# All loops of a five-engine kernel (GRU and selective scan over images) written out as straight code

## What is computed

```python
x = x + _L0_conv_ref(_gn(x), Wx, bx, Wh, bh, Wp)          # a GRU over the 196 positions
x = x + _L1_conv_ref(_gn(x), in_proj_w, conv_w, ...)      # a selective scan in 4 directions
# L0, at each of 196 positions, for all 32 images at once:
h_zrn = h @ Wh.T + bh
z = sigmoid(x_z + h_z); r = sigmoid(x_r + h_r)
ncand = tanh(x_n + r * h_n)
h = (1.0 - z) * ncand + z * h
# L1, in each of 4 directions, 192 channels, 16 states:
h = h * exp(d_t * A) + (d_t * u_t) * B_t ;  y = sum over states of h * C_t
```

## Time and profile before

| | us |
|---|---|
| median of three runs | 3238.71 (3237.17 to 3238.81) |
| the profiled execution's own time | 3240.27 |
| its span, first to last instruction | 3238.3 |
| TensorE busy in matmuls / weight loads | 2779.2 (86%) / 2070.2 (64%) |
| VectorE busy | 2672.7 (83%) |
| GpSimd busy | 2243.0 (69%) |
| ScalarE busy | 1824.2 (56%) |

### The profile page before, as it was taken

The page is one execution under the profiler, slowest core; times in us unless marked ns, Lnnn a source line. Parts: engine busy times, 40 slices in busy tenths (PEclk is TensorE's granted clock), DMA queues, the critical chain, the costliest instruction groups (busy, mean ns, idle before and its releaser), DMA issues.

```text
span 3238.3 us, 101526 instructions
## 1 busy us (share of the span) xinstructions
PE 2779.2 (86%) x39496; PEld 2070.2 (64%) x39496; DVE 2672.7 (83%) x4226; ACT 1824.2 (56%) x3872; POOL 2243.0 (69%) x1878
## 2 busy tenths in 40 slices
PE   4999999999996788888888888888888888888886
PEld 4999999986664555555555555565555655656554
DVE  6444444445776999999999999999999999999995
ACT  1111111112224677777777777777777777777773
POOL 5333333320005989989899898888989898898983
PEclk9999999999997999999999999999999999999999
DMA  5000000002334555545545555455454554555541
GB/s 199 0 0 0 0 0 0 0 5 97 112 112 140 156 156 153 153 156 149 177 140 163 159 144 169 141 160 174 134 170 149 157 163 140 162 161 155 162 146 46
DMA packets 57085, 385.29 MB, mean 119 GB/s; under 512 B 10100, under 2 KB 15060, under 8 KB 31700
## 3 DMA queue, kind: packets, MB, share of 16 engines
q1 hardware_dynamic: 57044, 384.79, 38.8%
HBM read 352.64 MB, written 32.11 MB: 119 GB/s over the span
## 4 chain that ended last, share of the span: by engine, by line
DVE 30%; PE 25%; issue 23%; POOL 16%; ACT 3%; DMA 1%; DVEq 1%; POOLq 0%; SPq 0%; ACTq 0%
DVE arena L776 15%; PE ps L1112 10%; PE ps L1121 9%; POOL arena L495 9%; DVE arena L779 9%; PE ps L1108 2%; DVE arena L793 1%; DVE conv_out L203 1%; POOL arena L471 1%; POOL arena L464 1%; POOL arena L468 1%; DVEq L773 1%; DMA x_in<-x_pair 1%; POOL arena L477 1%; POOL arena L482 1%
## 5 line engine op out<-in xcount | busy, mean ns | idle before, releaser
L1244 PE MATMUL ps<-arena,ident 128*128 128x392 f32 (+1 forms) x4096 | 1163.0, 417 | 0.9 <-DVE arena L788 0.9
L963 ACT ACTIVATE ps<-arena,abias,a 128x390 f32<-128x390 f32 x1024 | 690.0, 677 | 317.4 <-DVE arena L779 179.8
L788 DVE TENSOR_TENSOR arena<-arena,ps 128x784 f32<-128x784 f32 x768 | 745.7, 971 | 38.2 <-PE ps L1234 12.8
L1244 PEld LDWEIGHTS ps<-arena,ident 128*128 128x128 f32 x4096 | 682.8, 191 | 143.9 <-DVE arena L788 1.2
L776 DVE TENSOR_TENSOR_SCAN arena<-ps,arena 128x392 f32<-128x392 f32 x768 | 702.6, 956 | 7.4 <-POOL arena L495 6.3
L779 DVE TENSOR_TENSOR_SCAN arena<-ps,arena 128x392 f32<-128x392 f32 x768 | 702.6, 956 | 0.0
L1234 PE MATMUL ps<-arena,sel 96*128 96x196 bf16 x3072 | 391.6, 250 | 355.7 <-DVE arena L788 355.7
L1234 PEld LDWEIGHTS ps<-arena,sel 96*128 96x128 bf16 x3072 | 227.5, 97 | 665.0 <-DVE arena L788 630.7
L967 ACT ACTIVATE ps<-arena,abias,a 128x195 f32<-128x195 f32 x1024 | 477.7, 505 | 254.2 <-DVE arena L776 139.8
L495 POOL TENSOR_TENSOR arena<-arena 128x784 f32<-128x784 f32 x256 | 472.7, 1851 | 102.6 <-PE ps L1244 97.3
L495 POOL TENSOR_TENSOR arena<-arena,wx_sb 128x784 f32<-128x784 f32 x256 | 465.4, 1850 | 14.4 <-POOL arena L482 13.7
(11 more groups left out here) (175 smaller groups left out, 3295.4 us busy)
## 6 DMA issues: line engine op xcount, KB each, us to landing
wx_sb<-b_by_state SPq DMA_DIRECT2D x64, 1568.0 KB, 6.3
wh_sb<-b_by_state SPq DMA_DIRECT2D x64, 1568.0 KB, 6.3
arena<-b_by_image SPq DMA_DIRECT2D x128, 784.0 KB, 9.1
arena<-x_seq SPq DMA_DIRECT2D x4, 2352.0 KB, 15.9
x_in<-x_pair SPq DMA_DIRECT2D x16, 588.0 KB, 4.2
x_dram<-x SPq DMA_DIRECT2D x16, 588.0 KB, 2.8
x<-x_dram SPq DMA_DIRECT2D x16, 588.0 KB, 10.0
out<-xhat SPq DMA_DIRECT2D x16, 588.0 KB, 2.8
```

Of the source, the lines that this page charges most:

```text
L788: dve.tensor_tensor(h, h, bank(3), ALU.mult).then_inc(s["readout_ready"], 1)
L963: ins = act.activation(r, src, ACT.Exp, scale=a01[:, c:c + 1], bias=abias01[:, c:c + 1])
L1244: mm = pe.matmul(ps[:, 5 if g < 8 else 6, 0:cols], ident[:, :], h[:, m * cols:(m + 1) * cols], start=(opens and m == 0), stop=(closes and ...
```

## The change

In all fourteen places a loop on the engine becomes a loop of Python, so each round is put into the program as its own instructions: four loops of the recurrence (97 or 98 rounds, two steps each), a loop on each of the five engines in the middle stage (13 to 15 rounds) and one on each in the scan (14 rounds). `i` is then a number, the waits compare with constants, the addresses are constants, and branches and register instructions are gone. The operations, their order on each engine, the buffers and the waits are the same. With numbers alone, three helpers lose their second form.

```diff
@@ sync
-            with sp.Fori(2, PAIRS) as i:
+            for i in range(2, PAIRS):
...
-            with nc.Fori(1, PAIRS - 1, engines=[sp.engine], hint_back_edge=True) as i:
+            for i in range(1, PAIRS - 1):
                 pair(i, False, False)
@@ gpsimd
             def tok(t):
-                return seq[:, :, bass.ds(t, 1)].rearrange("p c o -> p (c o)") if not isinstance(t, int) else seq[:, :, t]
+                return seq[:, :, t]
...
-            with pool.Fori(0, T // 2 - 1) as i:
+            for i in range(0, T // 2 - 1):
                 for p in range(2):
                     norm(i * 2 + (p + 2), p)
                     keep(i * 2 + p, p)
...
-            with pool.Fori(1, PAIRS) as i:
+            for i in range(1, PAIRS):
                 rstd_c(i)
@@ vector
-            with dve.Fori(1, T // 2) as i:
+            for i in range(1, T // 2):
                 for p in range(2):
                     step(i * 2 + p, p)
...
-            with dve.Fori(2, PAIRS) as i:
+            for i in range(2, PAIRS):
                 norm_and_convolve(i)
@@ scalar
-            with act.Fori(0, T // 2) as i:
+            for i in range(0, T // 2):
                 for p in range(2):
                     step(i * 2 + p, p)
...
-            with act.Fori(3, PAIRS) as i:
+            for i in range(3, PAIRS):
                 conv_silu(i - 2)
                 xh_and_z(i - 1)
                 normalise(i)
@@ tensor
-            with pe.Fori(0, T // 2 - 1) as i:
+            for i in range(0, T // 2 - 1):
                 for p in range(2):
                     step(i * 2 + p, p)
...
-                        rhs = seq[:, col:col + 2, :] if isinstance(i, int) else seq[:, bass.ds(col, 2), :]
+                        rhs = seq[:, col:col + 2, :]
...
-            with pe.Fori(2, PAIRS) as i:
+            for i in range(2, PAIRS):
                 project(i)
@@ helper
 def dram(t, i):
-    return t[i] if isinstance(i, int) else t[bass.ds(i, 1), :, :].rearrange("o p c -> (o p) c")
+    return t[i]
```

More of the change, by code:

```diff
@@ L535, in _ @@
             pair(0, True, False)
-            with nc.Fori(1, PAIRS - 1, engines=[pool.engine], hint_back_edge=True) as i:
+            for i in range(1, PAIRS - 1):
                 pair(i, False, False)
@@ L807, in _ @@
             pair(0, True, False)
-            with nc.Fori(1, PAIRS - 1, engines=[dve.engine], hint_back_edge=True) as i:
+            for i in range(1, PAIRS - 1):
                 pair(i, False, False)
@@ L1071, in _ @@
             pair(0, True, False)
-            with nc.Fori(1, PAIRS - 1, engines=[act.engine], hint_back_edge=True) as i:
+            for i in range(1, PAIRS - 1):
                 pair(i, False, False)
@@ L1373, in _ @@
             pair(0, True, False)
-            with nc.Fori(1, PAIRS - 1, engines=[pe.engine], hint_back_edge=True) as i:
+            for i in range(1, PAIRS - 1):
                 pair(i, False, False)
```

## The result

The straight kernel takes 3391.91 us (median of four runs, 3390.32 to 3393.77) against 3238.19 (3237.17 to 3238.81, four runs of before on the same chip): ratio 1.0475, 95% interval 1.0457 to 1.0493. That is +153.7 us, where +138 was forecast. The profiled execution took 3392.38 us, +152.1 on that of before.

| stretch | before | after | change | forecast |
|---|---|---|---|---|
| start to the end of the recurrence | 719.3 | 882.0 | +162.6 | +145 |
| middle stage, to the first scan | 303.5 | 301.4 | -2.1 | -5 |
| the 16 pairs of the scan | 2180.1 | 2173.9 | -6.2 | -2 |
| tail after the last scan | 35.4 | 33.2 | -2.2 | none |

A forecast was written before the change was run, and what follows sets the result against it. The prediction took TensorE to bound the recurrence, with VectorE busy 1874.9 of the scan's 1909.7 us. Terms 145 - 5 - 2 = +138 us on 3238.7 gave 3377 us; range 3300 to 3430, held at 0.80.

The forecast's parts named there:

- Recurrence, fetch: Recurrence on TensorE: 225 instruction blocks fetched one after another, 3.63 us each, 817 us in place of 671.7: +145 us.
- The upper end (3.88): Recurrence: slowest block spacing allowed for, 3.88 us, giving 873 us for 225 blocks, +201.
- Recurrence, branches: Recurrence: 97 branches of 0.05 us saved would be 5 us, but counted as 0 where fetches set the pace.
- Middle stage: 14 looped rounds: the load of x issues sooner without branch and registers, 14 x 0.35 = -5 us.
- Scan: 14 looped pairs and the last pair: shorter VectorE idle spots, together -2 us; ends -13 and +25.
- The 0.08 of L788: Scan: VectorE's first wait for TensorE in a looped pair falls from 0.29 to 0.21 us, 14 x 0.08 = -1 us.
- VectorE's spot of 0.88 us: Scan, last pair: idle time after "issue", read as a late VectorE block after the loop; should go, -1 us.
- rival 3: Recurrence fetch-bound and VectorE's block boundaries in the scan cost +25 in place of -2: 3404 us; within fetch-bound's 0.84.
- Rivals 1: Recurrence: fetches keep up with TensorE, so only savings of 12 us stay: 3227 us, faster; chance 0.09.
- 2 (3241): Recurrence: each new block briefly holds the sequencer, fetches not serial; 14 us less 12, 3241 us, the same; chance 0.07.
- The signs that I had named: Recurrence: q8 packets 3.6 us apart, 300 or more in all, "issue" holes at different places, granted clock 1.00.
- TensorE's busy share: Recurrence: TensorE's busy share was to fall from 1.00 to about 0.8.

The follow-up runs named there:

- e1: Kernel after with one loop put back, TensorE's loop over the recurrence: 3233.53 us, ratio 0.9981.
- e2: Kernel before with only TensorE's loop over the recurrence written out: 3385.71 us, ratio 1.0449.
- e3: Kernel after with one more float32 matmul, its result unread, in each of the 196 recurrent steps: 3397.06 us, ratio 1.0481.
- e4: Kernel before with one more float32 matmul, its result unread, in each of the 196 recurrent steps: 3383.33 us, ratio 1.0444.
- e7: Kernel before with the first 98 steps of TensorE's recurrence written out and the rest looped: 3311.35 us, ratio 1.0230.
- e5: Kernel before with six steps instead of two per round of TensorE's recurrence loop, last four steps straight: 3242.16 us, ratio 1.0012.
- e6: Kernel before with fourteen steps per round of TensorE's recurrence loop, 13 rounds, last fourteen steps straight: 3440.97 us, ratio 1.0626.
- e9: Kernel before with only the five loops of the scan written out: 3232.43 us, ratio 0.9980.
- e11: Kernel before with only TensorE's loop of the scan written out: 3238.48 us, ratio 1.0000.
- e8: Kernel after with TensorE's recurrence as a loop of six steps a round, all other loops written out: 3235.75 us, ratio 0.9993.

## Why the prediction was right, and where its sizes were off

**Recurrence, fetch: right in kind, 17 us too small.** The term that was mis-sized is the time of a block. The sum took 225 blocks by 3.63 us; the stage lasted 225 by 3.71, which are the missing 17.6 us. The 3.63 came from two spacings, 3.68 and 3.58, where 220 have the mean 3.70 (and 3.62 to 3.69 in other traces). The upper end (3.88) was wide enough. That the time goes into serial fetching is shown in five ways: the one loop alone brings the loss and its absence removes it (e1, e2), extra work is nearly free inside it (e3, e4), the loss scales with the straight steps (e7), a longer body that stays resident has none of it (e5), and one that doesn't has all of it, registers and branches or not (e6).

The rule of the Trainium skill that I weighed, "Runtime: NRT & Kernel Launch", section "Instruction fetch mechanics", would have the crossing mostly hidden. For VectorE, ScalarE, GpSimd and SyncE, and for TensorE outside the recurrence, these runs agree (e1, e9 and e11 lose nothing). For TensorE at 86 instructions per us they don't: 3.70 us a block against a need of 2.98. Another page of the Trainium skill, "Advanced Engine Details and Errata", section "ISA Cache", gives TensorE 128 KB in two lines. The runs show that 6.9 blocks of 16.4 KB stay and 16.1 don't. That fits the size, but not two lines of one block each, since far more than two blocks stayed. Where between 6.9 and 16.1 the limit lies wasn't tried. Fetching ran one block ahead at any place that I looked at.

**Recurrence, branches: right.** Nothing came back there. e5 measured the price where TensorE is the limit: 3 us for 64 branches fewer, 0.05 each.

**Middle stage: -5 forecast, -2 measured.** The load came 0.50 us earlier, where 0.46 was worked out, and the wait ahead of L696 fell by 5.4 us in all. The step that failed is to take this wait as the one that closes the round. TensorE's averages behind L696 close it too: VectorE waits 4.2 us more for them ahead of L709. TensorE is busy for 217 of these 14 rounds' 226.4 us, so little could be gained, and 2.0 us of its 9.2 us of idle time were.

These 2 us are the code's. The 14 rounds take 226.4 us before and 224.5 after, 224.5 in e1 and 224.4 in e8, which have the same straight code, and 226.2 to 226.9 in the eight other traces with these loops. In e3, straight too, they take 226.2, but only there does a stretch at half clock (3.4 us) fall into them. The first round hides the gain in e1, whose whole stage is as long as before: it takes 18.2 to 18.3 us in the six traces where TensorE's clock is at its half level for 10.2 us within it (before and after among them), and 19.4 to 19.9 in the seven where it is so for 13.7 (e1 among them), with loops and without. The medians are too coarse for 2 us: e1 has everything that e9 has and the middle stage too, and is no faster.

**Scan: -2 forecast, -6 measured.** The 0.08 of L788 was right. What the sum did not have is that L793 is slowed by GpSimd's L495, and less once GpSimd's loop is straight. VectorE's spot of 0.88 us after "issue" at L776 is gone, as foreseen, and with it a second one of 0.25 us where the loop is entered. Their row in the trace of before, which after doesn't have:

```profile
DVE arena L776 <- issue: 1.1, 2, 0.9
```

So 14 x 0.37 = 5.1 us in the looped pairs, 0.3 from the first pair to the loop, and 0.8 in the last pair (0.88 less an L793 that is longer there): the 6.2. The +25 of rival 3 didn't occur; with straight code VectorE met no late block.

**Tail: not in my sum, -2.2.** TensorE's clock was at its half level for 10.2 us from 3220.7 before and for 6.8 us from 3373.9 after; a group of four matmuls (L1294) takes 1.51 us at that level and 0.83 at the full one. The code isn't the cause: the tail took 35.2 to 35.6 us in the three traces with 10.2 us of half clock (before, e3, e11) and 32.9 to 33.2 in nine of the ten with 6.8 (34.7 in e4), and both groups hold looped and straight scans.

Sum: 162.6 - 2.1 - 6.2 - 2.2 = 152.1 us between the profiled executions. The total came out nearer (14 us off) than its largest term (17.6) by luck: gains in the scan and the tail that I had not foreseen cancel a part. Rivals 1 (3227) and 2 (3241) are out. The signs that I had named held: packets 3.70 us apart, one at a time, 309 in all, holes "issue" at a different place each step, and the granted clock at 1.00. Only TensorE's busy share (0.88, not 0.8) didn't: the modelled end of a matmul ahead of a hole counts as busy.

## What to carry to other kernels

Count the instructions per microsecond of an engine's tightest stretch, and compare the time for one block (256 instructions on TensorE) with the spacing of the "instruction" packets, here 3.7 us: below it, straight code is bound by fetching, and no busy share or semaphore says so. Keep such a stretch in a loop whose body stays resident (6.9 blocks did, 16.1 did not), and remember that each first pass and each straight tail pays as well. Where the engine has slack, straight code is free and may give a little: with the five scan loops alone written out, 3232.43 us, 0.2% faster than the kernel before and the fastest of all here, level with the kernel after with its one loop put back (3233.53).

## What the runs showed that I had not expected

- VectorE's L793 (scalar_tensor_tensor, 128x588) takes 0.77 us alone, 1.05 to 1.08 where it overlaps GpSimd's L495 for some 0.45 us, and 1.39 where it overlaps for 0.76. Whichever begins second pays: L495 takes 1.85 us beside an L793 that began behind it and without one, but an L471 that began 0.05 us behind an L793 took 2.01 in place of 1.43.
- A jump back to a block that isn't resident costs 3.0 to 3.6 us, more than the longest hole of straight code in the kernel after (1.4), and a loop that doesn't fit is slower (3440.97) than no loop (3385.71).
- The extra matmul that costs 144 us in the loop costs 5 in the straight kernel.
- The same code gives stages that differ by some 2 us from one execution to the next, by how long TensorE's clock stays at its half level behind the recurrence and in the tail. A gain of that size in one trace is no gain until further traces repeat it.
